# Probabilities as the stationary operand, in two rounded parts with a ones column in the context, in a Perceiver layer on one core

## What is computed

```python
q = rmsnorm((layernorm(x) @ Wq).reshape(B, Sq, H, D), gq)
k = rmsnorm((ctx @ Wk).reshape(B, Skv, H, D), gk)
v = (ctx @ Wv).reshape(B, Skv, H, D)
attn = softmax(einsum('bqhd,bkhd->bhqk', q, k) / sqrt(D))
x = x + einsum('bhqk,bkhd->bqhd', attn, v).reshape(B, Sq, H * D) @ Wo
```

## Time and profile before

| | |
|---|---|
| median of 3 runs | 1527.63 us (1527.08 to 1528.84) |
| the profiled execution, its own time | 1526.53 us |
| its span, first to last instruction | 1524.8 us |
| queries, first to last matmul | 22.9 to 132.5 us |
| cross attention, first transpose to last weighing | 139.1 to about 1286.8 us |
| the rest, to the end | about 238 us |
| granted TensorE clock, mean of the span | 0.982 |

### The profile page before, as it was taken

One profiled execution on the slowest core, in us unless ns is written; L12 is line 12 of the kernel. 1 busy time (PEld: TensorE's weight loads), 2 busy tenths in 40 slices (PEclk: granted clock), 3 DMA queues, 4 the chain that ended last, 5 costly groups with the idle time before them and its releaser, 6 DMA issues. The chain is left out here.

```text
span 1524.8 us, 29153 instructions
## 1 busy us (share of the span) xinstructions
PE 1438.0 (94%) x6176; PEld 973.3 (64%) x6176; DVE 1300.6 (85%) x2093; ACT 1156.1 (76%) x4810; POOL 942.6 (62%) x1474
## 2 busy tenths in 40 slices
PE   5996999999999999999999999999999999976886
PEld 3664666666666666666666666666666666853554
DVE  6876888998988898889888998988998988765985
ACT  5886888787888887788878787887878877534763
POOL 4001778887878887788878787878887876010000
PEclk9998999999999999999999999999999999996998
DMA  3000000000000000000000000000001011000000
GB/s 139 37 1 1 1 1 23 7 17 17 8 22 2 23 1 22 2 22 1 22 2 22 10 13 21 3 22 2 23 1 47 1 49 42 1 1 0 8 7 15
DMA packets 9818, 25.05 MB, mean 16 GB/s; under 512 B 736, under 2 KB 6016, under 8 KB 9520
## 3 DMA queue, kind: packets, MB, share of 16 engines
q1 hardware_dynamic: 9648, 23.49, 4.3%
HBM read 22.44 MB, written 1.05 MB: 15 GB/s over the span
## 5 line engine op out<-in xcount | busy, mean ns | idle before, releaser
L807 PE MATMUL psK<-wkh,c_cTh 128*124 128x512 f32 x832 | 509.2, 612 | 6.1 <-DVE c_prod L1235 2.8
L1235 DVE TENSOR_TENSOR c_prod<-psK,c_c 124x512 f32<-124x512 f32 x624 | 427.0, 684 | 65.6 <-PE psK L807 61.7
L1529 POOL TENSOR_TENSOR c_acc<-c_acc,c_prob 123x1024 f32<-123x1024 f32 (+1 forms) x192 | 459.1, 2391 | 2.6 <-issue 1.4
L827 PE MATMUL psO<-c_prob,raw 123*128 123x512 f32 (+1 forms) x832 | 424.9, 591 | 0.0
L1021 ACT ACTIVATE c_unused<-c_prod 124x128 f32<-124x128 f32 x832 | 247.5, 299 | 110.5 <-DVE c_prod L1235 110.5
L1252 DVE TENSOR_TENSOR c_prob<-psS,c_ss 124x512 f32<-124x512 f32 x416 | 286.9, 690 | 50.2 <-PE psS L818 34.8
L807 PE MATMUL psK<-wkl,c_cTh 128*124 128x512 f32 x832 | 328.6, 395 | 0.0
L1027 ACT ACTIVATE c_prob<-c_prob,shift 124x1024 f32<-124x1024 f32 x208 | 238.9, 1149 | 56.7 <-DVE c_prob L1252 45.4
L1242 DVE TENSOR_REDUCE c_ss<-c_prod 124x8 f32<-124x1024 f32 x208 | 253.8, 1220 | 7.2
L1013 ACT ACTIVATE c_unused<-psK 124x128 f32<-124x128 f32 x832 | 218.8, 277 | 52.9 <-PE psK L807 37.4
L807 PEld LDWEIGHTS psK<-wkh,c_cTh 128*124 128x124 f32 x832 | 154.4, 186 | 143.6 <-issue 88.7
(11 more groups left out here) (312 smaller groups left out, 2311.5 us busy)
## 6 DMA issues: line engine op xcount, KB each, us to landing
raw<-in_ctx SPq DMA_DIRECT2D x16, 799.5 KB
raw<-in_L_xattn_Wq SPq DMA_DIRECT2D x3, 512.0 KB, 9.7
xs<-in_x SPq DMA_DIRECT2D x1, 1024.0 KB, 5.7
big<-in_L_xattn_Wk SPq DMA_DIRECT2D x1, 1024.0 KB, 9.0
c_prod<-in_L_xattn_Wo SPq DMA_DIRECT2D x1, 1024.0 KB, 5.2
out<-s_y SPq DMA_DIRECT2D x8, 128.0 KB, 1.7
big<-in_L_ffn_W_qkv SPq DMA_DIRECT2D x1, 768.0 KB, 12.9
c_wqkv<-in_L_attn_W_qkv SPq DMA_DIRECT2D x1, 768.0 KB, 15.9
```

Source lines behind the costliest of these rows:

```text
L807: last = nc.tensor.matmul(psK[0:ROWS, c % 2, :], x[:, slot, :], w[:, cols], start=(n == 0), stop=(n == len(terms) - 1))
L827: nc.tensor.matmul(psO[:, half, :], raw[0:rows, b, tile, :], prob[0:rows, probs(v), half * BANK:(half + 1) * BANK], start=(tile == 0), sto ...
L1235: nc.vector.tensor_tensor(prod[:, k % 2, c - GRAM, :].rearrange("p (h c) -> p h c", c=CD), psK[0:ROWS, c % 2, :].rearrange("p (h c) -> p h ...
L1529: nc.gpsimd.tensor_tensor(acc[0:rows, batch % 2, :], acc[0:rows, batch % 2, :], prob[0:rows, probs(s), :], ALU.add).then_inc(S.acc, 1)
```

## The change

- **Weighing.** The probabilities are split by ScalarE (high part, a copy of 1024 columns) and GpSimd (low part, a subtraction of 1024 columns) and become the stationary operand, in blocks of 128 columns (two heads by 64 queries). The context moves: 130 columns, its 128 and two columns of ones (`CW`), so that the sum of the probabilities comes out beside the weighed context. For each tile there are 8 blocks and 3 rounded matmuls to a block: high by context high (130 columns), low by context high (130), high by context low (128). The blocks stand in three banks (psO's two and psM) as `BLOCKS`; on a batch's first tile the first matmul of each bank is widened to the whole bank's 390 or 260 columns, to start it.
- **Denominators.** Accumulator, matmuls by ones, logarithm, exponential, Newton step and the multiplication by GpSimd go. Instead VectorE takes a reciprocal of the ones' column and multiplies by it, once for each bank at a batch's end (`normalise`). The result is transposed by TensorE in 8 blocks over three later steps and copied out by ScalarE.
- **Order.** A step works on six tiles (v, h, s, r, k, x), with the splitting of the probabilities a stage of its own (h), and TensorE's order in a step is new. ScalarE sums two heads of chunk 1 instead of four, VectorE ten heads instead of eight. Semaphores are one for each chunk and half. Tiles are taken from the context's buffer backwards (`place`).
- **Queries.** The squares are split by GpSimd into two rounded parts, and two rounded matmuls of 512 columns replace the full float32 one. It is issued an item later, behind the six matmuls of the next-but-one item. VectorE makes the low part of three quarters of Wq, GpSimd clears the buffer in four pieces between items, and the last quarter of Wq lies in `big`.
- **Loads.** A context buffer is loaded again once it is transposed and its low part made; the attention's W_qkv is loaded late, into the context's buffer.

The core of the diff:

```diff
 def weigh...
-                nc.tensor.matmul(psO[:, half, :], raw[0:rows, b, tile, :], prob[0:rows, probs(v), half * BANK:(half + 1) * BANK],
-                                 start=(tile == 0), stop=(tile == NT - 1)).then_inc(S.vmm, 1)
-            def denominators(i, batch, half):
...
-                nc.tensor.matmul(den_bank(i, batch, half), T.ones[0:ROWS, :], acc[:, batch % 2, half * BANK:(half + 1) * BANK],
-                                 start=True, stop=True).then_inc(S.den, 1)
+            def weigh(i, v, n):
...
+                if n == 0:
+                    pe.wait_ge(S.probl, done(i, v, 1))
...
+                if tile == 0:
+                    pe.wait_ge(S.norm, batch_done(i, batch - 1, len(BLOCKS), n + 1))
+                bank = BANK_ORDER[n]
+                for m, block in enumerate(BLOCKS[bank]):
+                    cols = slice(block * P, (block + 1) * P)
+                    out = banks[bank][:, m * CW:(m + 1) * CW]
+                    if tile == 0 and m == 0:
+                        width = len(BLOCKS[bank]) * CW
+                        nc.tensor.matmul(banks[bank][:, 0:width], probh[0:rows, v % 2, cols], ch_wide[0:rows, place(v) * CW:place(v) * CW + width], start=True, stop=False)
+                    else:
+                        nc.tensor.matmul(out, probh[0:rows, v % 2, cols], ch[0:rows, place(v), :], start=False, stop=False)
+                    nc.tensor.matmul(out, probl[0:rows, probs(v), cols], ch[0:rows, place(v), :], start=False, stop=False)
+                    last = nc.tensor.matmul(out[:, 0:CD], probh[0:rows, v % 2, cols], low[0:rows, place(v), :], start=False, stop=(tile == NT - 1 and block == BLOCKS[bank][-1]))
+                last.then_inc(S.vmm, 1)
 TensorE's step, now:
+                (transpose of x), turn_out, score_half(i, s, 0), weigh(i, v, 0), key_chunk(i, k, 3), weigh(i, v, 1),
+                key_chunk(i, k, 0), weigh(i, v, 2), score_half(i, r, 1), key_chunk(i, x, 1), key_chunk(i, x, 2)
 ScalarE:
+            def probabilities_high(i, h):
+                act.wait_ge(S.expd, done(i, h, 1))
+                act.wait_ge(S.vmm, done(i, h - 2, len(BLOCKS)))
+                nc.scalar.activation(probh[:, h % 2, :], prob[:, probs(h), :], ACT.Copy).then_inc(S.probh, 1)
 VectorE:
+            def normalise(i, batch, n):
...
+                nc.vector.reciprocal(inverse[:, first:first + count].unsqueeze(2), sums[:, :, CD:CD + 1]).then_inc(S.inv, 1)
...
+                nc.vector.tensor_tensor(weighted[:, first * P:(first + count) * P].rearrange("p (m c) -> p m c", c=CD), sums[:, :, 0:CD],
+                                        over(inverse[:, first:first + count], CD), ALU.mult).then_inc(S.norm, 1)
 GpSimd:
-                    nc.gpsimd.tensor_tensor(acc[0:rows, batch % 2, :], acc[0:rows, batch % 2, :], prob[0:rows, probs(s), :], ALU.add).then_inc(S.acc, 1)
+            def probabilities_low(i, h):
+                pool.wait_ge(S.probh, done(i, h, 1))
+                nc.gpsimd.tensor_tensor(probl[:, probs(h), :], prob[:, probs(h), :], probh[:, h % 2, :].bitcast(F32), ALU.subtract).then_inc(S.probl, 1)
 queries, TensorE and GpSimd:
-                    nc.tensor.matmul(psS[:, m % 2, :], T.ones[:, :], square[:, m % 2, :], start=True, stop=True).then_inc(S.total, 1)
+                    nc.tensor.matmul(psS[:, o % 2, :], onesr[:, :], squareh[:, o % 2, :], start=True, stop=False)
+                    nc.tensor.matmul(psS[:, o % 2, :], onesr[:, :], squarel[:, o % 2, :], start=False, stop=True).then_inc(S.total, 1)
+                nc.gpsimd.tensor_tensor(squareh[:, m % 2, :], square[:, m % 2, :], blank[:, :].broadcast_to([P, BANK]), ALU.add).then_inc(S.squareh, 1)
+                nc.gpsimd.tensor_tensor(squarel[:, m % 2, :], square[:, m % 2, :], squareh[:, m % 2, :].bitcast(F32), ALU.subtract).then_inc(S.squarel, 1)
```

More of the change, by code:

```diff
@@ new lines, in weigh @@
+            def weigh(i, v, n):
+                batch, tile, rows = v // NT, v % NT, rows_of(v)
+                if n == 0:
+                    pe.wait_ge(S.probl, done(i, v, 1))
+                    for piece, tiles in enumerate(PIECES):
+                        if tile == tiles.start:
+                            pe.wait_ge(S.nat, batch_done(i, batch, len(PIECES), piece + 1))
+                    if v == 0:
+                        pe.wait_ge(W.unit, BLANK // P + 2)
+                if tile == 0:
+                    pe.wait_ge(S.norm, batch_done(i, batch - 1, len(BLOCKS), n + 1))
[11 more added lines that the diff above has]
+                last.then_inc(S.vmm, 1)
@@ L844, in step, with turn_out @@
+            def turn_out(i, batch, part):
+                pe.wait_ge(S.norm, batch_done(i, batch, len(BLOCKS)))
+                for m, block in enumerate(BLOCKS[part]):
+                    last = nc.tensor.transpose(psT[:, (m + 1) * P:(m + 2) * P], weighted[:, block * P:(block + 1) * P], T.ident[:, :])
+                last.then_inc(S.turned, 1)
+            def step(i, v, h, s, r, k, x):
+                part = turning(v)
                 if x is not None:
@@ L875, in step, with turn_last @@
                     turn(1)
+            def turn_last():
+                pe.wait_ge(W.vTl, 2)
+                pe.wait_ge(S.norm, batch_done(LAST, 1, len(BLOCKS)))
+                for bank, half in ((psT, 0), (psM, 1)):
+                    for m in range(HB):
+                        block = half * HB + m
+                        last = nc.tensor.transpose(bank[:, m * P:(m + 1) * P], weighted[:, block * P:(block + 1) * P], T.ident[:, :])
+                    last.then_inc(W.lastT, 1)
             def turn(q):
@@ new lines, in step @@
+            def step(i, v, h, s, r, k, x):
+                finished = v is not None and v % NT == NT - 1
+                if s is not None:
+                    scale_scores(i, s, 1)
+                if x is not None:
+                    dve.wait_ge(S.cth, done(i, x, 1))
+                    dve.wait_ge(S.s0, done(i, x - before(CT_SLOT, x), 1))
+                    nc.vector.tensor_tensor(cTl[:, CT_SLOT[x % TP], :], psT[:, 0:ROWS], cTh[:, CT_SLOT[x % TP], :].bitcast(F32),
+                                            ALU.subtract).then_inc(S.ctl, 1)
+                if finished:
+                    normalise(i, v // NT, 0)
+                if k is not None:
+                    products(i, k, 3)
@@ L1484, in begin @@
                     context_twice_low(0, 0, 0)
-                if n in (1, 2):
-                    query_low(0, 0, n - 1)
+                if n == 1:
+                    for half in range(2):
+                        query_low(0, 0, half)
                 if n in (2, 3, 4):
```

537 lines of the change are left out of this document (267 added, 270 removed).

## The result

| | before | changed |
|---|---|---|
| median | 1527.36 us (4 runs, 1526.41 to 1528.84) | 1764.56 us (4 runs, 1759.91 to 1767.74) |
| ratio | | 1.1545, 95% interval 1.1522 to 1.1567 |
| profiled execution, its own time and span | 1526.5, 1524.8 | 1766.73, 1765.0 |

A forecast was written before the change was run, and what follows sets the result against it. TensorE was taken to bound the kernel: 1526.5 us + 185 (tiles) + 3.5 (last tile) + 0 (queries) + 1 (setup) = 1716, 1717 us as a median. The range 1695 to 1750 us holds nine tenths of the likeliest case (85%).

The forecast's parts named there:

- +0.889: TensorE's step in the cross attention: 24 small matmuls and output transposes come, weighing halves and denominators go; +0.889 us a tile.
- +3.5 of the text: Last tile: weighing waits for the exponential, ScalarE's copy and GpSimd's low part; paid only once, +3.5 us.
- 185 of the text: Cross attention: the longer TensorE step taken over all 208 tiles, +185 us.
- 189.5 in the sum: Whole kernel: cross attention +185, last tile +3.5, queries 0 and setup of ones and zeros +1 us.
- Rivals A and B: Weighing's small matmuls: A, loads hide, under 0.074 us each, 1460 us, 3%; B, in-between price 0.085, 1585 us, 4%.
- From 16 to 256 columns the price hardly moves: it is the load of 128 columns of weights that is paid: Weighing's small matmuls: moving columns hide under the weight load, 0.1115 us each, 2.676 us for 24.
- Rival C: Chain from root to weighing across four engines: a late ScalarE copy makes TensorE wait before L904, 1800 us, 8%.
- slack of 1.2 us: Cross attention step: TensorE's 6.33 us covers every other engine, by 1.2 us in the tightest case.
- So a tile costs what TensorE needs for its step: Cross attention: TensorE, busy 70.57 of 71 us, sets the time of a tile, 5.442 us before the change.
- only TensorE's own work counts: Cross attention step: no waits to win; prices of TensorE's work sum to 5.48 us against 5.442 measured.
- Clearing the buffer and the loads of context have two dozen us to spare: cover, no cost.: Context buffer: clearing and loading it have two dozen us to spare, so they add 0 us.
- Queries: Queries phase: TensorE's possible 13 us gain lost as VectorE waits for GpSimd; 0 us, ends -13 and +20.

The follow-up runs named there:

- unrolled_pe: The changed kernel with TensorE's loop over the seven pairs written out, same instructions in the same order, early context load kept: 1724.23 us, ratio 1.1285.
- two_terms: late_load without the product of the probabilities' low parts with the context, so 16 small matmuls a tile instead of 24: 1569.65 us.
- late_load: The changed kernel with a context load waiting again for the last weighing of its batch instead of the batch's last transpose: 1761.82 us.
- unrolled_late: unrolled_pe with late_load's line, so the batch-0 context load starts away from the other engines' jump: 1722.06 us beside 1725.24 us for a copy of unrolled_pe.
- before_extra: The kernel before with one more transfer of 0.74 MB in each iteration, lying across the loop's jump: 1548.75 us, ratio 1.0137.

## Why the prediction was right and wrong

**What bound.** Right. TensorE bound before and after. Weighing, transposes and the rest cost in the step what the sum said: +0.889 forecast; 6.334 - 5.442 = 0.892 by unrolled_pe's transposes. The spans close: the first transpose 3.3 us later (142.4 against 139.1), 207 distances 184.7 us, from the last transpose to the end 268.1 against 259.2, so 8.9 us. The last number is larger than the +3.5 of the text because the weighings run five steps behind the transposes: five of the 208 (5 x 0.889 = 4.4 us) fall there. (The 207 distances hold that many fewer, so all the weighings together cost 184.7 + 4.4 = 189 us and not the 185 of the text.) In all 196.9 = 1721.7 - 1524.8, against 189.5 in the sum.

**Rivals A and B.** Both refuted at their point of decision. No load hid: 0.111 apart in a stream of thousands, unchanged at half the columns, 0.063 at half the weights. "From 16 to 256 columns the price hardly moves: it is the load of 128 columns of weights that is paid" was the reading that carried the forecast, and the runs bear it out.

**Rival C.** Refuted: 1.0 us of idle time before L904, and GpSimd's L1599 at 2.39 us as forecast. The stage h and the slack of 1.2 us held.

**The step that failed.** "So a tile costs what TensorE needs for its step" and "only TensorE's own work counts", and with it the product +0.889 x 208. It takes all 208 steps as alike. Six of them begin with a jump, and the change takes TensorE's body from 1,056 to 2,112 matmuls and loads. The sum has no term for that. I asked what the 24 matmuls and their 24 loads cost in the array, and not what they do to the length of the loop and to its fetching; the page of before has the queue to ask of, q8 with 21 packets in the whole run. Measured in its place: 40.3 us (1764.56 - 1724.23), and 43.3 between the two profiled executions (1765.0 - 1721.7). TensorE's idle time at the jumps is 16.3 us of it. The rest is the clock behind the stalls, here in the 30 us from each of the six jumps on (busy, granted clock, DMA share, GB/s):

```profile
393.00:423.00 30.00, 28.51 (x154) 0.83 0.01 2
566.00:596.00 30.00, 29.00 (x185) 1.00 0.01 3
734.00:764.00 30.00, 28.92 (x156) 0.83 0.01 3
906.00:936.00 30.00, 28.08 (x143) 0.77 0.01 3
1080.00:1110.00 30.00, 27.94 (x142) 0.77 0.01 3
1254.00:1284.00 30.00, 28.16 (x142) 0.77 0.01 3
```

In unrolled_pe all six stretches have 1.00. A clock of 0.83 over 30 us loses 5.1 us and one of 0.77 loses 6.9, together 31 us, and behind one jump nothing is lost. 16.3 + 31, less the 2.6 us that TensorE waits in unrolled_pe, makes 44.6 against the 43.3 between the profiled executions. A page of the Trainium skill would have put me on it: Runtime: NRT & Kernel Launch (Instruction fetch mechanics) gives TensorE room for 2,048 instructions, fetched in blocks of 256, and says that a branch to one outside what is held stalls. By that room alone the changed body (2,198 instructions) doesn't fit and the old one (1,231) does, as the trace shows; 1,782 should still have fitted, and two_terms fetched it anew. (The same section speaks of a window of two blocks; by that before's body would stall too, and it does not.) The measured limit lies between 1,366 and 1,782 instructions, 1,280 and 1,696 of them matmuls and loads. What sets it was not tested.

**"Clearing the buffer and the loads of context have two dozen us to spare: cover, no cost."** I asked only whether the load arrives in time, not what it meets. It crosses the jump and holds ScalarE 3.6 and GpSimd 4.3 us at most; that it delays the fetching of their instructions fits this and was not tested apart. Here it cost some 3 us, if anything (late_load and unrolled_late, whose runs overlap with their partners'), since TensorE is the one that binds, and 21 us in the kernel before, where TensorE waits for ScalarE (before_extra). It was my first explanation of the missing 47 us, and late_load took it away: all engines stood still in the profile, and the ones that the load held weren't the ones that mattered.

**Queries.** Forecast 0, within -13 to +20; measured +4.7. The saved TensorE time does not show, as the text expected, and something more is lost: an item takes 3.43 us on the mean (ScalarE's squares start from 24.8 to 131.0 us) against 3.30 in before (24.7 to 126.9), 4.0 us in 31 items. The root pass stretched, as the text feared (median 0.680 to 0.800 us, at most 1.527), which agrees with VectorE waiting for GpSimd; the lower granted clock of TensorE may have a part too. How the loss divides between them was not tested.

**Sum.** 189.5 forecast + 4.7 queries + 40.3 at the jump = 234.5, against 237.2 measured; the weighings' 4 us more than forecast, above, are of the size of what is left.

## What to carry to other kernels

Price a matmul with new weights each time by the load: at up to about as many moving columns as loaded ones (64 and 130 against 128 here, and 256 cost hardly more), narrowing what moves wins nothing, so the operand that changes less often, or is needed in fewer pieces, belongs on the weights' side. When a change multiplies instructions inside a loop, count the engine's body and look at its instruction queue: here packets that came back in each iteration went with a stall at the jump and mostly a slow clock behind it, and writing out that engine's loop took both away. Keep large transfers away from the jump, also when the body fits.

## What the hardware showed that I had not expected

- A TensorE stall of 2.4 to 2.9 us at a jump costs about twice as much again by the clock: 5.1 to 6.9 us in the 30 us behind it (0.50 for 10 us and more), though not each time (1.00 behind one of six).
- TensorE's body of 1,280 matmuls and loads (1,366 instructions) is not fetched anew at the jump (q8: 22 packets in the run), one of 1,696 (1,782) is (79), one of 2,112 (2,198) too (88).
- A transfer of 0.74 MB across the jump raises ScalarE's wait there from 1.1 to 4.3 us at most, and it makes a kernel 21 us slower whose TensorE body fits and in which the data queue takes 5.2% of the DMA engines' time (before_extra).
- Small matmuls in rounded float32: 0.111 us with 128 columns of weights, be it 64 or 130 columns that move; 0.063 us with 64 columns of weights and 130 moving.
